# Tridiagonalisation of a 1024 x 1024 matrix on one core: panels written out, and the first step of a panel begun before the trailing update has ended

## The reference, cut to what matters

```
deg  = A.sum(0) + A.sum(1) - diag(A)
L    = d_inv_sqrt[:, None] * (diag(deg) - A) * d_inv_sqrt[None, :]
_, U = eigh(L)
agg  = einsum('mn,bnd->bmd', U.T, features)   # then two small products, and U @ out
```

## Time and profile before

| | |
|---|---|
| median of 3 executions | 9222.39 us |
| the profiled execution, its own time | 9224.03 us |
| its span, first to last instruction | 9222.3 us |
| DVE, PE, ACT, POOL busy, share of the span | 73%, 62%, 29%, 13% |
| tridiagonalisation | from about 830 to 5830 us of the span |
| granted TensorE clock in it | 0.83 of full speed |

### The profile page before, as it was taken

One profiled execution on the slowest core, in us unless ns is written; L12 is line 12 of the kernel. 1 busy time (PEld: TensorE's weight loads), 2 busy tenths in 40 slices (PEclk: granted clock), 3 DMA queues, 4 the chain that ended last, 5 costly groups with the idle time before them and its releaser, 6 DMA issues. The chain is left out here.

```text
span 9222.3 us, 334698 instructions
## 1 busy us (share of the span) xinstructions
PE 5701.9 (62%) x138962; PEld 3872.5 (42%) x138962; DVE 6703.0 (73%) x32749; ACT 2708.2 (29%) x7811; POOL 1214.8 (13%) x5408
## 2 busy tenths in 40 slices
PE   5696778777788877777776554344434330036956
PEld 2364555555566666655665544101000000033446
DVE  3566666677677777777778888888888889954055
ACT  1442111111111111111113334566666650010046
POOL 0000111111122222222223333100000000000000
PEclk8898999999999999888665555555555555578989
DMA  1000000000000000000000000000000000000000
GB/s 38 1 1 20 4 4 4 4 4 4 4 4 4 4 4 4 4 4 4 4 4 4 4 4 4 1 0 0 0 0 0 0 0 0 0 0 1 0 19 19
DMA packets 24662, 42.83 MB, mean 5 GB/s; under 512 B 2464, under 2 KB 20128, under 8 KB 23200
## 3 DMA queue, kind: packets, MB, share of 16 engines
q1 hardware_dynamic: 23200, 21.70, 0.7%
HBM read 17.50 MB, written 4.19 MB: 2 GB/s over the span
## 5 line engine op out<-in xcount | busy, mean ns | idle before, releaser
L313 PE MATMUL tri_y<-L 128*32 128x256 f32 (+7 forms) x36792 | 1976.5, 345 | 11.8 <-issue 10.9
L313 PEld LDWEIGHTS tri_y<-L 128*32 128x32 f32 x36792 | 1195.6, 122 | 226.5 <-issue 50.6
L405 ACT ACTIVATE tri_mu<-tri_ring,tri_tiny 128x1 f32<-128x1 f32 x1022 | 267.1, 261 | 1985.4 <-PE tri_ring L296 1985.4
L1536 PE MATMUL ev_pairs<-ev_sgn,ident 128*128 128x448 bf16 x1024 | 428.8, 574 | 579.7 <-ACT ev_sgn L1501 579.7
L1660 DVE SCALAR_TENSOR_TENSOR ev_seq<-ev_seq,ev_rowG,ev_u 128x112 f32<-128x112 f32 x2048 | 682.8, 333 | 91.0 <-DVE ev_u L1645 2.3
L408 ACT ACTIVATE tri_sM<-tri_half_M,tri_s 128x8 f32<-128x8 f32 (+5 forms) x767 | 229.0, 299 | 1464.7 <-DVE tri_s L601 1464.7
L1645 DVE TENSOR_TENSOR ev_u<-ev_shifted,ev_seq 128x112 f32<-128x112 f32 x2048 | 560.4, 274 | 86.6 <-DVE ev_seq L1667 14.0
L1490 ACT ACTIVATE ev_shifted<-ev_x,ev_rowG 128x112 f32<-128x112 f32 x2112 | 613.0, 372 | 31.4 <-DVE ev_rowG L1617 31.4
L296 PE MATMUL tri_ring<-L 128*32 128x32 f32 (+25 forms) x35704 | 599.6, 206 | 3.3 <-issue 3.1
L296 PE MATMUL tri_k<-tri_kp,tri_half 128*32 128x1 f32 x6136 | 191.1, 184 | 615.3 <-DVE tri_x L609 614.8
L296 PEld LDWEIGHTS tri_ring<-L 128*32 128x32 f32 x35704 | 516.0, 118 | 3.7 <-issue 3.7
(11 more groups left out here) (660 smaller groups left out, 14148.8 us busy)
## 6 DMA issues: line engine op xcount, KB each, us to landing
adj<-in_adj_dram SPq DMA_DIRECT2D x12, 1024.0 KB, 8.1
x<-in_x_dram SPq DMA_DIRECT2D x8, 512.0 KB, 7.2
out_dram<-x SPq DMA_DIRECT2D x8, 512.0 KB, 6.6
gcn_w<-in_L_gnn_W_dram SPq DMA_DIRECT2D x2, 128.0 KB, 2.2
spec_w<-in_L_gnn_W_dram SPq DMA_DIRECT2D x2, 64.0 KB, 1.8
dot_wt<-in_L_gnn_W_dram SPq DMA_DIRECT2D x1, 64.0 KB, 1.8
dot_rows<-in_L_gnn_b_lin_dram SPq DMA_DIRECT2D x1, 64.0 KB, 2.7
dot_rows<-in_L_gnn_b_dram SPq DMA_DIRECT2D x1, 64.0 KB, 3.4
```

The costliest lines, as they stand in the source:

```text
L313: last = nc.tensor.matmul(y[32 * g:32 * g + 32, 0:T * 32], A[:, b + t, XC:XC + 1].broadcast_to([P, 32]), cols, start=(t == 0), stop=(t == ...
L405: nc.scalar.activation(mu[:, :], sigma, ACT.Sqrt, bias=tiny[:, :]).then_inc(root_ready, 1)
L1536: last = nc.tensor.matmul(sums[h], S["ident16"][:, :], sgn[:, h * (GRP // 2) + k:(h + 1) * (GRP // 2) + k, :].rearrange("p s w -> p (s w)" ...
```

## The change: what it does

1. **Panels written out.** `bodies` has one entry for each of the 32 panels, and the loops of the engines become Python loops over one iteration. No branch is left in the stage.
2. **The first step's norm, pivot, root and inverse are moved ahead of the additions.** DVE takes the norm of the next panel's first x right after the old panel's last step (into a semaphore `first_part`). ACT writes the four shifted tables right after the last reflector (`tables`), before it copies `PTa`. PE makes pivot and norm (`first_step`) between its transposes and the chunk products; the norm's sum goes to `sigma_v`, for `ring` is in use by the update. ACT takes the root (`first_root_of`) after its `PTa` copy, and DVE does five more instructions to the inverse (`first_pair`) between its `PTb` copy and the first addition. The step's own code has these under `if r:` now.
3. **ACT's four saves** (L425 to L428) move from before its `PTa` copy to behind the root.
4. **The first product waits tile by tile.** `product(t)` of a first step waits until the additions of its own row tile are made, not for the table `Cw`. On PE it stands behind all chunk products. Only ACT's `Cw` copy still waits for all additions; POOL waits for `Cw`. DVE's wait for `window_ready` goes, but for the first panel.

```diff
-        bodies = [(0, 0, 1, 1, NB_P), (0, 1, LP - 1, 0, NB_P)] + [(b, 0, LP, 0, NB_P) for b in range(1, NT - 1)] \
-            + [(NT - 1, 0, LP - 1, 0, NB_P), (NT - 1, LP - 1, 1, 0, NB_P - 1)]
+        bodies = [(b, p, 1, 1 if b == p == 0 else 0, NB_P - 1 if (b, p) == (NT - 1, LP - 1) else NB_P) for b in range(NT) for p in range(LP)]
...
+            def first_step(k):
+                b, s = bodies[k][0], bodies[k][3]
+                pe.wait_ge(tables_ready, k + 1)
+                pe.wait_ge(first_part, k + 1)
+                four(pivot(s), Hw[:, s, 0:1].broadcast_to([P, 32]), A[:, b, XC - 1:XC + 1])
+                four(sigma_v, ones[:, 0:32], part[:, :]).then_inc(first_norm, 1)
+
+            def rows_updated(k, t):
+                if k == 0:
+                    return 1
+                m = bodies[k][0] + t - bodies[k - 1][0]
+                return 1 + chunks_before[k - 1] + sum(c[0] <= m for c in chunks(bodies[k - 1][0]))
...
-                with pe.Fori(0, cnt) as it:
+                for it in range(cnt):
                     pn = it + panels_before[k]
-                    pe.wait_ge(window_ready, pn + 1)
-                    pe.wait_ge(updated, it * per_chunks[k] + (chunks_before[k] + 1))
+                    if k == 0:
+                        first_step(k)
...
                         def product(t):
+                            if r == 0:
+                                pe.wait_ge(updated, rows_updated(k, t))
...
                         last.then_inc(turned, 1)
+                    pe.wait_ge(panel_done, pn + 1)
+                    first_step(k + 1)
                     pe.wait_ge(turned_copied, pn * 2 + 2)
...
+            def first_root_of(k):
+                act.wait_ge(first_norm, k + 1)
+                nc.scalar.activation(mu[:, :], sigma_v, ACT.Sqrt, bias=tiny[:, :]).then_inc(first_root, 1)
...
                     act.wait_ge(updated, it * per_chunks[k] + (chunks_before[k] + 1))
-                    act.wait_ge(saved, pn * 4 + 1)
-                    nc.scalar.activation(Hw[:, :, 0], ident[:, bass.ds(r0, NB_P)], ACT.Copy)
-                    nc.scalar.activation(hot2[:, :], ident[:, bass.ds(r0, NB_P)], ACT.Copy, scale=0.5)
-                    nc.scalar.activation(Mw[:, :, 0], low[:, bass.ds(r0, NB_P)], ACT.Copy)
-                    nc.scalar.activation(half_M[:, :, 0], low[:, bass.ds(r0, NB_P)], ACT.Copy, scale=0.5)
                     nc.scalar.activation(Cw[:, b:NT, :], A[:, b:NT, bass.ds(i0, NB_P)], ACT.Copy).then_inc(window_ready, 1)
...
                     if k != last_body:
+                        act.wait_ge(w_ready, W)
+                        tables(k + 1)
                         act.wait_ge(turned, pn * 2 + 1)
...
+                        first_root_of(k + 1)
+                    act.wait_ge(panel_done, pn + 1)
...
...
+            def first_pair(k):
+                b, s = bodies[k][0], bodies[k][3]
+                f1 = fl[:, s:s + 1]
+                dve.wait_ge(first_root, k + 1)
+                kk = mark(V_.reciprocal(rt[:, :], mu[:, :]))
+                k_sg = mark(V_.tensor_scalar(sg[:, :], pivot(s)[:, 1:2], 0.0, -0.5, ALU.is_ge, ALU.add))
+                after(kk)
+                kk = mark(V_.scalar_tensor_tensor(out=S2[:, :], in0=rt[:, :], scalar=sigma_v, in1=mu[:, :], op0=ALU.mult, op1=ALU.add))
...
+                V_.reciprocal(inv[:, :], pair[:, s, :]).then_inc(inv_ready, 1)
...
+                    if k != last_body:
+                        dve.wait_ge(x_ready, s1 - s0)
+                        norm(bodies[k + 1][0], first_part)
                     kappas = kbank[:, s0:s1]
...
                     last.then_inc(turned_copied, 1)
+                    dve.wait_ge(tables_ready, pn + 2)
                     for numbers_ in step_ranges:
                         dve.sem_clear(numbers_)
+                    links = 0
+                    first_pair(k + 1)
                     for i, (m, c0, w) in enumerate(chunks(b)):
```

More of the change, by code:

```diff
@@ L325, in _ @@
                                 product(t)
[L326 to L327 removed]
+                        if r:
+                            pe.wait_ge(norm_part, r)
+                            four(sigma, ones[:, 0:32], part[:, :]).then_inc(norm_ready, 1)
                         if few(T):
[L329 removed]
+                            if r:
+                                four(sigma_v, ones[:, 0:32], part[:, :]).then_inc(norm_again, 1)
                             for t in range(first):
@@ L380, in _, with tables @@
             pe.wait_ge(last_ready, 4)
-            four(sigma, ones[:, 0:32], part[:, :]).then_inc(norm_ready, 1)
+            four(sigma, ones[:, 0:32], part[:, :]).then_inc(last_norm, 1)
             for c in range(2):
                 last = nc.tensor.matmul(ring[2 + c][:, :], ones[:, :], DS[:, c * 512:(c + 1) * 512], start=True, stop=True)
-            last.then_inc(norm_ready, 1)
+            last.then_inc(last_norm, 1)
         @block.scalar
         def _(act):
+            def tables(k):
+                rows_ = slice(bodies[k][1] * NB_P, (bodies[k][1] + 1) * NB_P)
+                nc.scalar.activation(Hw[:, :, 0], ident[:, rows_], ACT.Copy)
+                nc.scalar.activation(hot2[:, :], ident[:, rows_], ACT.Copy, scale=0.5)
+                nc.scalar.activation(Mw[:, :, 0], low[:, rows_], ACT.Copy)
+                nc.scalar.activation(half_M[:, :, 0], low[:, rows_], ACT.Copy, scale=0.5).then_inc(tables_ready, 1)
+            def first_root_of(k):
+                act.wait_ge(first_norm, k + 1)
+                nc.scalar.activation(mu[:, :], sigma_v, ACT.Sqrt, bias=tiny[:, :]).then_inc(first_root, 1)
             act.wait_ge(low_ready, 7)
+            act.wait_ge(start_ready, 7)
             for k, (b, it0, cnt, s0, s1) in enumerate(bodies):
                 T = NT - b
-                with act.Fori(0, cnt) as it:
+                for it in range(cnt):
                     pn = it + panels_before[k]
@@ L452, in _, with mark, after, norm @@
             V_.tensor_tensor(A[:, 0, XC:XC + 1], A[:, 0, XC:XC + 1], low[:, 0:1], ALU.mult).then_inc(updated, 1)
+            links = 0
+            def mark(ins):
+                nonlocal links
+                links += 1
+                ins.then_inc(chain, 1)
+                return links
+            def after(m):
+                dve.wait_ge(chain, m)
+            def norm(b, ready):
+                X = xcol(b)
+                V_.tensor_tensor_reduce(out=x2[:, b:NT], in0=X, in1=X, scale=1.0, scalar=0.0, op0=ALU.mult, op1=ALU.add,
+                                        accum_out=part[:, 0:1]).then_inc(ready, 1)
+            def first_pair(k):
[6 more added lines that the diff above has]
+                kk = mark(V_.scalar_tensor_tensor(out=S2[:, :], in0=rt[:, :], scalar=sigma_v, in1=mu[:, :], op0=ALU.mult, op1=ALU.add))
+                ins = V_.tensor_scalar(f1, pivot(s)[:, 1:2], pivot(s)[:, 1:2], sigma_v, ALU.mult, ALU.is_lt)
+                if few(NT - b):
+                    ins.then_inc(fl_ready, 1)
+                elif s:
+                    mark(ins)
+                else:
+                    ins.then_inc(Bn_ready, 1)
+                after(kk)
+                after(k_sg)
+                kk = mark(V_.scalar_tensor_tensor(out=pair[:, s, :], in0=S2[:, :].broadcast_to([P, 2]), scalar=sg[:, :], in1=pivot(s), op0=ALU.mult, op1=ALU.add))
+                after(kk)
+                V_.reciprocal(inv[:, :], pair[:, s, :]).then_inc(inv_ready, 1)
+            dve.wait_ge(updated, 1)
+            norm(0, first_part)
+            first_pair(0)
             for k, (b, it0, cnt, s0, s1) in enumerate(bodies):
@@ L456, in _ @@
                 act_t = slice(b, NT)
-                with dve.Fori(0, cnt) as it:
+                for it in range(cnt):
                     pn = it + panels_before[k]
-                    links = 0
-                    def mark(ins):
-                        nonlocal links
-                        links += 1
-                        ins.then_inc(chain, 1)
-                        return links
-                    def after(m):
-                        dve.wait_ge(chain, m)
-                    dve.wait_ge(window_ready, pn + 1)
-                    def norm(r):
-                        if r:
-                            dve.wait_ge(x_ready, r)
-                        X = xcol(b)
-                        V_.tensor_tensor_reduce(out=x2[:, act_t], in0=X, in1=X, scale=1.0, scalar=0.0, op0=ALU.mult, op1=ALU.add,
-                                                accum_out=part[:, 0:1]).then_inc(norm_part, 1)
-                    if norm_first(T):
-                        norm(0)
+                    if k == 0:
+                        dve.wait_ge(window_ready, 1)
                     for s in range(s0, s1):
@@ L555, in _ @@
                             if s + 1 < s1:
-                                norm(r + 1)
+                                dve.wait_ge(x_ready, r + 1)
+                                norm(b, norm_part)
```

127 lines of the change are left out of this document (65 added, 62 removed).

## The result

The kernel after takes 9052.13 us in the median of 4 executions (9033.67 to 9059.01). On the same chip the kernel before took 9215.71 us (4 executions, 9206.53 to 9224.98). The ratio is 0.9819, with a 95% interval of 0.98 to 0.9838.

The account below looks back on a forecast made before the run. No engine alone bounds it; the gain must come from 218.5 us between last addition and next x over 31 boundaries. 127.5 us gained less 3 is 124.5 off, giving 9098 us, range 9068 to 9126.

Parts of the forecast that it names:

- this sum: Time from last addition to the next panel's first x over 31 boundaries, 218.5 us; all gain must come from it.
- the clock theory: Later steps, from the experiments: without PE's idle time at the boundary its clock stays up; otherwise they stay within 10 us.
- Part 1's price: Panel starts behind loop heads: writing them out saves 1.95 us a time, some 43 us for 22 heads.
- two sentences on control flow: Loop heads: compare-and-branch of about 108 ns, 2.4 us for 22, against a target fetch after each taken branch; second favoured.
- The sum behind the last addition: Last addition to next first x, all boundaries: of 218.5 us, 127.5 were to go.
- The product: First product after a boundary: at T = 8, 64 matmuls in 5.60 or 3.67 us, x at E + 5.84 or E + 3.91.
- the fast rate: PE's product matmuls at 57.3 ns each, taken for first products with T of 8 to 6.
- E: The end of the last addition at a panel boundary, from which both later chains are timed.
- the slow rate: PE's product matmuls at 87.5 ns each, taken for first products with T = 5.
- The chain of `Cw`: From last addition through table `Cw` and POOL to x: 2.44 us a boundary, the later chain for T of 4 and less.
- What is put ahead of the additions: Norm, root and inverse work before the first addition: 0.1 us a boundary, 3 us in all, bounds 0 and 29.
- Rival A: Steps behind 15 boundaries with T of 5 or more: clock holds there too, 25 us more go, 9073 us; chance 0.18.

Follow-up runs that it names:

- experiment 1: The kernel before with its 32 panels written out and nothing else changed: 9141.06 us, ratio 0.991.
- experiment 2: The kernel after, but every tile of a first product waits for all additions: 9085.85 us, ratio 0.9851.
- experiment 3: experiment 1 plus 40 unread matmuls (20 for T of 3 and 4) behind each panel's chunk products: 9137.91 us, ratio 0.9915.
- experiment 4: The kernel after with DVE's five instructions from root to inverse moved behind the additions: 9061.6 us, ratio 0.9826.
- experiment 5: experiment 1 with two DVE copies of 1024 columns before the first norm at the 22 former loop heads: 9181.48 us, ratio 0.9959.
- experiment 9: The kernel after with POOL's first xm of a panel waiting for the first addition, not for table Cw: 9071.76 us, ratio 0.9836.
- experiment 8: The kernel after with eight unread matmuls per step also for T of 8 and 7, and twelve instead of ten for T of 3: 9042.61 us, ratio 0.9809.
- experiment 10: The kernel after with the changes of experiment 8 and experiment 9 together: 9042.73 us, ratio 0.9806.

## Why the prediction was wrong

**The step that failed** stands in the first part: "inside the panels' later steps the same instructions stand in the same order", and from it "All that the change can win must come out of this sum". The same instructions in the same order took 31.7 us less, 26.0 over both pairs of profiles. That sentence closed off 4487 of the stage's 4975 us. It makes 32 of the 49 us by which the span's gain (173.5) passed the forecast (124.5); the stretches behind the last addition make 12, the way ahead of its end 4, the rest of the kernel 1.

**What took its place.** That it is the written-out code, not the early product, is shown: without matmuls added in the steps, written-out code has 4455.7 to 4470.6 us in eight profiles, 4462 in the mean (experiments 1 to 5 and 9 and the kernel after twice), against 4487.5 and 4482.3 in loops. Where in the steps it lies can be read from the traces. For each later step with T of 8 to 3 I took the time from x to x, less that of the quickest step at full clock with the same T at the same place of a panel, in any of the fourteen profiles (at two places with T = 3 there is none). Summed over the steps that had some time at the clock's lower level, this is 73 and 65 us in loops and 43 to 59 (mean 52) written out. Over the steps at full clock it is 44 and 50 in loops and 39 to 43 (mean 41) written out. With T of 2 and 1, where all steps run at 0.50, nothing is gained. So of the 23 us in the mean some 17 come from steps that no longer fall to the lower level, with T = 4 (6 us), 7 (5) and 8 (3) above all, and some 6 from the steps at full clock. PE's code alone has 50 and 45 us, DVE's 56 and 49.

So the clock theory was wrong in its condition and right in the main term. Why the clock falls less often behind written-out boundaries stays open. PE's idle time there does not settle it: in the kernel after there is none before the first product, and still the four steps behind the third boundary with T = 7 took 27.74 us at 0.75.

The other candidate was that in a loop of four panels the engines meet the same place of their code at the same step in each turn. The timeline of the kernel before shows such a place, the product of one step and that of the next:

```profile
1366.23 3.21 PE L313 MATMUL tri_y<-L 128*32 128x256 f32 x54
...
1372.38 1.47 PE L313 MATMUL tri_y<-L 128*32 128x256 f32 x20
1374.06 2.32 PE L313 MATMUL tri_y<-L 128*32 128x256 f32 x34 [0.21 <-issue]
```

The 54 matmuls take 3.21 us in one step and 4.00 in the next, with 0.21 us idle in the middle, in which PE waited for nothing that the profile shows. The step is 0.79 us longer, and the same step is long by 0.5 to 0.8 us in all three turns. Two fetches of 16384 bytes of instructions began in it, but a fetch of the same size also began 0.15 us into the product that took 3.21 us, so that the fetches cause the long step is not shown. In the written-out kernels such steps are there too, but stand elsewhere in each panel. They can carry no more than the 6 us of the steps at full clock. PE's idle time from issue in front of this product does not speak even for that: it is about as long in written-out code (the second row, experiment 1) as in loops (the first), and 14.1 us with PE's code alone written out:

```profile
PE tri_y L313 <- issue: 10.9, 20, 1.4
...
PE tri_y L312 <- issue: 10.1, 22, 0.8
```

What the written-out code does save is fetches at the heads. The page of the kernel before and that of experiment 1 differ by 44 fetches of 16384 bytes, two for each of the 22 heads:

```profile
q8 instruction: 1117, 18.30, 0.8%
...
q8 instruction: 1073, 17.58, 0.8%
```

PE's code alone written out also brings this number to 1073; with DVE's alone it stays at 1117. So these are fetches of PE's code.

**Part 1's price** failed with it. "1.95 us a time, some 43 us for 22 loop heads" was the difference of two stretches with T = 3, taken for all. Behind the last addition experiment 1 gave 62.3 us (218.5 to 156.2), for the heads cost more with T of 7 to 4, and the change in the later steps belongs to this part, too: 78 us by the medians, where 43 were forecast. I had priced the heads by DVE's row alone. Of the two sentences on control flow that I weighed, the trace had decided rightly: the price is not that of a compare-and-branch. The Trainium skill, Runtime: NRT & Kernel Launch, Instruction fetch mechanics, names a stall behind a taken branch, and the traces agree: DVE idle for up to 4.6 us in front of the first norm, PE for up to 4.0 in front of the pivot, and neither in experiment 1. The same section of the Trainium skill calls the crossing from one block of straight code to the next mostly hidden; the 0.79 us of the step above may be such a crossing or not, no run here decides it.

**The sum behind the last addition.** It was to keep 91.0 us (218.5 less 127.5) and keeps 79.2. That the two are so near is in part luck, for two errors stand against each other: the heads gave 62.3 us where 43 were taken, and the rest of the change 77.0 (156.2 to 79.2) where 84.5 were left. By its terms:

- *The product* was right. 64 matmuls at the fast rate were to take 3.67 us and take 3.66; x was to be there at E + 3.91 and is at E + 3.83. With T = 7 it is 3.0 (3.45 forecast) and with T = 6 2.4 (2.99): the matmuls with fewer columns are faster, which I had called an upper estimate. With T = 5 two of four are at the granted clock of 0.50 and take 3.6 (3.74 forecast), the others 2.9 and 2.2. The reason given for the slow rate there, that the whole block was at the lower level, was misread from the boundaries: its later steps ran at 0.93 to 0.98 before.
- *The chain of `Cw`* was the right chain, as z's wait for POOL's Bc at T = 4 shows, and mis-sized: 2.44 us forecast, 2.03 to 2.30 measured, 33.8 us instead of 39.0 over the 16 boundaries with T of 4 and less. One term of it, ACT's 0.22 us behind the last addition, is 0.03 (1054.96 to 1054.99). It is 0.03 in experiment 1 too, at all 31 boundaries, so it went with the loops.
- *What is put ahead of the additions* was to cost 3 us. The copy-to-addition gap sums to 43.4 us where it was 46.9, and the whole way to the last addition is 1.4 us shorter. What the place is worth is 4.5 to 5.5 us behind the last addition (experiment 4).

**Rival A** named the later steps and 25 us, and its time, 9073, was the nearest. It was right that later steps would change from slow to fast, by about half its 25 us with T of 5 or more and by some 8 us with T = 4. Its condition (a boundary at which PE does not stop) falls with experiments 1 to 3: the later steps gain the same without the early product. The rule of the Trainium skill beside it, TensorE: Matmul & The Clock Gate, Loop structure matters more than you think, agrees with the trace in the first product (1.00 granted with T of 8 to 6); it does not carry into the steps behind, which ran at 0.75 behind one of the boundaries with T = 7.

By the medians of the runs the change divides so: panels written out 78 us, the first step's parts ahead of the additions 55 (experiment 1 to 2), tiles one by one 34.

## What to carry to other kernels

Where a change unrolls a loop, price it over the whole body, not at the head alone: read the idle time from issue of every engine that has the loop, since the latest of them sets the price and it is not the same one everywhere, and compare the steps behind the head by their granted clock, for they can change though no instruction in them does. Where an update ends in a chain that needs only its last piece, start what needs the earlier pieces beside it; with T = 8 that part could be forecast to 0.1 us from two timelines. A sum "by the same instructions" is a claim about time that needs a row of its own.

## What the runs showed of the hardware that was not expected

- A loop's head is dear on each engine by itself: DVE idle 4.19 us, PE up to 4.0 us before its first matmul, with two more 16384-byte fetches of PE's code a head (44 in all); 78 us in all for 22 heads on four engines, of which either engine's code alone gives 26 (PE) or 38 (DVE).
- Steps in which nothing was edited can change with the code around them: the same four steps with T = 7 took 27.66 us at a granted clock of 0.75 in the kernel before and 21.48 at 1.00 with PE's loop alone written out.
- Less time at TensorE's lower level counts by where it lies: 83 us less in experiment 3, all but 14 of them at the boundaries, gave nothing that can be seen; 58 us less in the later steps in experiment 8 went with 17.8 us of those steps.
- An edit that shortened its own stretch by 0.1 us a boundary went with 20 us more (experiment 9): in the block T = 7 16 later steps touched the lower level where the kernel after has 10, and none does with added matmuls in the steps (experiments 8 and 10). An edit worth less than some 20 us can hardly be judged by its time alone in this kernel. Why that kernel fell so is open.
